# One pass for the gate-weighted biases, one turn and two DMAs for the softmax maxima, new orders

## The reference

```
h = token_block(x)                        # five taps, relu, batch norm
h = h + softmax_attention(layernorm(h))   # 8 heads of 16, +0.1 on a band
h = h + top2_experts(layernorm(h))        # 8 experts, hidden 256, gelu
h = h + linear_attention(layernorm(h))    # causal, elu + 1, 8 heads
h = h + experts(causal_attention(layernorm(h)))   # 8 experts, hidden 512
```

## Time and profile before

| | |
|---|---|
| median of three runs | 4315.55 us (4314.95, 4315.55, 4320.37) |
| span of the profiled execution, first to last instruction | 4319.1 us |
| its own time from outside | not listed by itself; the nearest run is 4320.37 us |
| PE busy | 4066.8 us, 41344 matmuls |
| DVE, ACT, POOL busy | 3367.6, 2784.5, 2596.6 us |
| token block | about the first 160 us |
| full rounds | 30 of about 125.6 us |

### The profile page before, as it was taken

The page is one execution under the profiler, slowest core; times in us unless marked ns, Lnnn a source line. Parts: engine busy times, 40 slices in busy tenths (PEclk is TensorE's granted clock), DMA queues, the critical chain, the costliest instruction groups (busy, mean ns, idle before and its releaser), DMA issues.

```text
span 4319.1 us, 104773 instructions
## 1 busy us (share of the span) xinstructions
PE 4066.8 (94%) x41344; PEld 3009.8 (70%) x41344; DVE 3367.6 (78%) x8878; ACT 2784.5 (64%) x4796; POOL 2596.6 (60%) x2494
## 2 busy tenths in 40 slices
PE   7678999999999999999999999999999999999998
PEld 3346777777777777777777777777777777777766
DVE  3357888888888888888888888878888887888876
ACT  3235766666676666667666666766666676666654
POOL 2034666666666666666666666666666666666656
PEclk9779999999999999999999999999999999999999
DMA  4200000011100001110000111000101100010000
GB/s 149 68 27 28 18 18 29 28 30 30 30 19 24 22 28 30 30 30 18 23 23 28 30 30 30 23 26 16 30 28 30 30 23 26 16 30 28 28 16 6
DMA packets 136939, 127.62 MB, mean 30 GB/s; under 512 B 28928, under 2 KB 135360, under 8 KB 136448
## 3 DMA queue, kind: packets, MB, share of 16 engines
q1 hardware_dynamic: 136448, 120.91, 9.6%
HBM read 71.05 MB, written 49.55 MB: 28 GB/s over the span
## 4 chain that ended last, share of the span: by engine, by line
PE 56%; DVE 24%; ACT 6%; POOL 5%; issue 4%; DMA 3%; SPq 2%; ACTq 0%; DVEq 0%; POOLq 0%
PE pf L1301 9%; PE pf L1303 8%; PE pf L1302 8%; PE pa L1561 8%; DVE h L1285 4%; PE pa L1447 3%; DVE hid_hi L1266 3%; PE pa L1543 3%; PE pa L1346 2%; PE pa L1433 2%; POOL inv_norm L650 2%; PE pa L1301 2%; ACT xn L726 2%; PE pa L1641 2%; PE pa L1303 2%
## 5 line engine op out<-in xcount | busy, mean ns | idle before, releaser
L660 POOL TENSOR_TENSOR hid_lo<-hid,hid_hi 128x504 f16<-128x504 f32 x1536 | 1835.5, 1212 | 775.8 <-DVE hid_hi L1266 775.8
L886 ACT ACTIVATE hid<-pf,vec 128x504 f32<-128x504 f32 x1536 | 1014.7, 680 | 505.5 <-PE pf L1303 356.9
L1301 PE MATMUL pf<-w_hi,hid_hi 128*126 128x128 f16 x6144 | 1133.7, 224 | 10.7 <-DVE h L1285 10.2
L1303 PE MATMUL pf<-w_hi,hid_lo 128*126 128x128 f16 x6144 | 1115.8, 221 | 0.0
L1302 PE MATMUL pf<-w_lo,hid_hi 128*126 128x128 f16 x6144 | 1115.4, 221 | 0.0
L1301 PEld LDWEIGHTS pf<-w_hi,hid_hi 128*126 128x126 f16 x6144 | 844.1, 137 | 153.5 <-issue 53.2
L1302 PEld LDWEIGHTS pf<-w_lo,hid_hi 128*126 128x126 f16 x6144 | 843.8, 137 | 28.5 <-issue 0.2
L1266 DVE CAST hid_hi<-hid 128x504 f16<-128x504 f32 x1536 | 845.4, 573 | 8.2 <-ACT hid L886 2.7
L1303 PEld LDWEIGHTS pf<-w_hi,hid_lo 128*126 128x126 f16 x6144 | 845.2, 138 | 0.0
L1285 DVE SCALAR_TENSOR_TENSOR h<-pf,gates,h 126x128 f32<-126x128 f32 x2048 | 574.1, 342 | 155.2 <-PE pf L1303 152.6
L616 POOL TENSOR_TENSOR pt<-pt,band 126x262 f32<-126x262 f32 x512 | 351.2, 707 | 527.6 <-ACT pt L773 527.4
(11 more groups left out here) (208 smaller groups left out, 7486.8 us busy)
## 6 DMA issues: line engine op xcount, KB each, us to landing
qk_spread<-terms SPq DMA_DIRECT2D x224, 126.0 KB, 2.5
qk_spread<-terms SPq DMA_DIRECT2D x192, 63.0 KB, 2.3
y_scratch<-hid SPq DMA_DIRECT2D x32, 252.0 KB, 2.1
y_in<-y_scratch SPq DMA_DIRECT2D x32, 252.0 KB, 3.2
terms<-qk_hi SPq DMA_DIRECT2D x32, 252.0 KB, 2.5
terms<-qk_lo SPq DMA_DIRECT2D x32, 252.0 KB, 2.6
qk_spread<-terms SPq DMA_DIRECT2D x32, 252.0 KB
terms<-ot_hi SPq DMA_DIRECT2D x32, 252.0 KB, 2.4
```

The costliest lines, as they stand in the source:

```text
L660: nc.gpsimd.tensor_tensor(hid_lo[:, c % 8], hid[:, c % HIDS], hid_hi[:, c % 8], ALU.subtract).then_inc(hid_lo_done[c % 2], 1)
L886: nc.scalar.activation(hid[:, c % HIDS], pf[:, c % 2, 0:TOK], func, bias=vec[:, bias:bias + 1]).then_inc(F["hid_ready"], 1)
L1301: nc.tensor.matmul(out, ah, bh, start=start, stop=False, skip_group_check=skip)
L1303: return nc.tensor.matmul(out, al, bh, start=False, stop=stop, skip_group_check=skip)
```

## The change

*Maxima.* `minus_max` becomes a 128 x 128 tile, and the 16 heads and sequences of maxima are its first 32 columns. One f16 matmul with the identity turns all of it; ACT copies the 32 rows to SBUF as f16; SP places 16 rows of 126 values each into row 3, and the other 16 into row 67 of the query tile, by two DMAs. The second pass of the scores waits for both. The four additions on DVE go.

*Biases.* The gates are written three times side by side (96 columns). Turned, rows 0 to 31 and 64 to 95 are the f16 high part, rows 32 to 63 the low part, which DVE makes by a subtraction (`gate_low`). `b2` is f16, with its high part in rows 0 to 63 and its low part in rows 64 to 95, and its rows hold zeros but for the columns of their own tile. So one f16 matmul of 96 rows and 512 columns gives high x high, low x high and high x low of all four tiles. `b2` is loaded within the token block: POOL zeroes an f32 staging tile, SP loads 12 small blocks (three in each of four iterations), POOL copies to f16 and subtracts for the low part.

*Orders.* All fifteen strings are new; of these PE's round is shown. Some semaphores share a name and count higher; that changes no wait.

```diff
-PE_ROUND = ("lhhoalhhaoaoloahlohloaoohlhhlaooahlahohalolhalahllaaoolahollhholallhhalaaolaoloahhaolahhlhoohaoo"
-            "laahlhhlaohaoohlolqhoohalolaaohaoohhhoqqqlholhalhloqlolhlolollhhlooqlhhqololhhoohhoolll")
+PE_ROUND = ("hhlahooqhaloaolhahlooolhohlhhloqahlaohaoahoalhhloohalhallaaloohllaalallaloaaohloalhaohlqaolooohl"
+            "ahhlahhoalhlhooaolhaaahooollohahhhoaoqqlhhoholhllloolhholohalhllohlqohlqolohllhoohhlool")
...
         # SP, in the token block's loop
+            def load_b2(i):
+                sp.wait_ge(b2_step, 1)
+                for part in range(3):
+                    first = part * G_ROWS + i * EXPERTS
+                    sp.dma_start(b2_wide[first:first + EXPERTS, :, i], b2_dram).then_inc(small_loaded, 16)
...
                 load_x(k + 1, 1)
                 store_y(k, 1)
+                if EARLY < k <= EARLY + TILES:
+                    load_b2(k - EARLY - 1)
...
         # SP, softmax_attention
+                for _ in range(8):
+                    yield
+                sp.wait_ge(S0["max_copied"], n(p + 1))
+                for r in range(2):
+                    sp.dma_start(q16[0][64 * r + MAX_ROW:64 * r + MAX_ROW + 1].rearrange("o g (t q) -> o (g t) q", t=TILES),
+                                 max_rows[16 * r:16 * r + 16]).then_inc(max_sent, 16)
...
         # POOL, after the constants
+            pool.wait_ge(w_lo_done, PIECES)
+            nc.gpsimd.memset(b2_wide, 0.0).then_inc(b2_step, 1)
+            pool.wait_ge(small_loaded, 32 + 16 * 3 * TILES)
+            nc.gpsimd.tensor_copy(b2[:], b2_wide).then_inc(b2_step, 1)
+            pool.wait_ge(b2_step, 2)
+            low_rows = slice(2 * G_ROWS, 3 * G_ROWS)
+            nc.gpsimd.tensor_tensor(b2[low_rows], b2_wide[low_rows], b2[low_rows], ALU.subtract).then_inc(b2_step, 1)
...
         # ACT
-                nc.scalar.copy(gate_t[a][:], pa[a][:, GATES_T[a], 0:TILE]).then_inc(SS[a]["gate_t_ready"], 1)
+                nc.scalar.copy(gate_t[a][0:3 * G_ROWS], pa[a][0:3 * G_ROWS, GATES_T[a], 0:TILE]
+                               ).then_inc(SS[a]["gate_t_high"], 1)
...
+                act.wait_ge(S0["max_turned"], n(p + 1))
+                nc.scalar.copy(max_rows[0:TILES * HEADS], pa0[0:TILES * HEADS, 0, 0:TILE]
+                               ).then_inc(S0["max_copied"], 1)
...
         # DVE, in front of each addition of a bias, and without the four additions
+            def gate_low(a, p):
+                dve.wait_ge(SS[a]["gate_t_high"], n(p + 1))
+                part = slice(G_ROWS, 2 * G_ROWS)
+                nc.vector.tensor_tensor(gate_t[a][part], pa[a][part, GATES_T[a], 0:TILE], gate_t[a][part],
+                                        ALU.subtract).then_inc(SS[a]["gate_t_ready"], 1)
...
-                for g in range(GROUPS):
-                    dve.wait_ge(S0["max_turned"], n(p * 4 + g + 1))
-                    nc.vector.tensor_tensor(q16[0][:, g], pa0[:, g % 3, 0:TOK], q16[0][:, g],
-                                            ALU.add).then_inc(S0["q_shifted"], 1)
...
         # PE
+                nc.tensor.matmul(pa[a][0:TILE, BIAS2[a]], gate_t[a][0:3 * G_ROWS],
+                                 b2[0:3 * G_ROWS, a].rearrange("p t d -> p (t d)"), start=True,
+                                 stop=True).then_inc(SS[a]["bias2_ready"], 1)
...
+                nc.tensor.matmul(pa0[:, 0, 0:TILE], minus_max[0:TILE], ident16[0:TILE, 0:TILE], start=True,
+                                 stop=True).then_inc(S0["max_turned"], 1)
...
-                pe.wait_ge(S0["q_shifted"], n(p * 4 + 4))
+                pe.wait_ge(max_sent, n.plain((p + 1) * 32))
```

More of the change, by code:

```diff
@@ L303, in program @@
         lsum = [sb(f"lsum{i}", [128, TILES]) for i in range(2)]
-        gate_t = [sb(f"gate_t{i}", [128, TILE]) for i in range(2)]
+        gate_t = [sb(f"gate_t{i}", [128, TILE], F16) for i in range(2)]
         y_in = sb("y_in", [128, TOK])
@@ L507, in softmax_attention @@
                     load_y(p + 1)
-                for _ in range(A0_STEPS):
+                for _ in range(8):
[4 more added lines that the diff above has]
+                                 max_rows[16 * r:16 * r + 16]).then_inc(max_sent, 16)
+                for _ in range(A0_STEPS - 8):
                     yield
@@ L529, in _ @@
             load_y(0)
-            sp.wait_ge(consts_built, 1)
-            for i in range(TILES):
-                sp.dma_start(b2[i * EXPERTS:(i + 1) * EXPERTS, :, i], b2_dram).then_inc(small_loaded, 16)
             run_rounds(softmax_queries_and_keys, softmax_attention, linear_and_causal_attention, hidden, output,
@@ L765, in softmax_attention @@
             def softmax_attention(p):
-                for _ in range(9):
+                for _ in range(8):
                     yield
+                act.wait_ge(S0["max_turned"], n(p + 1))
+                nc.scalar.copy(max_rows[0:TILES * HEADS], pa0[0:TILES * HEADS, 0, 0:TILE]
+                               ).then_inc(S0["max_copied"], 1)
+                yield
                 for g in range(8):
@@ L1012, in gate_top2 @@
                 nc.vector.tensor_tensor(over[0:TILE], other, mine, ALU.is_gt)
-                nc.vector.tensor_tensor(same[0:TILE], other, mine, ALU.is_equal).then_inc(S0["ranks2"], 1)
-                dve.wait_ge(S0["ranks2"], n(p + 1))
+                nc.vector.tensor_tensor(same[0:TILE], other, mine, ALU.is_equal).then_inc(S0["rank_step"], 1)
+                dve.wait_ge(S0["rank_step"], n(p * 4 + 1))
                 flat = earlier[0:TILE].rearrange("p a b -> p (a b)").unsqueeze(1).to_broadcast(
@@ L1365, in gate_bias2 @@
                 pe.wait_ge(SS[a]["gate_t_ready"], n(p + 1))
-                for i in range(TILES):
-                    last = nc.tensor.matmul(pa[a][0:TILE, BIAS2[a], i * D:(i + 1) * D], gate_t[a][:], b2[:, a, i],
-                                            start=True, stop=True)
-                last.then_inc(SS[a]["bias2_ready"], 1)
+                nc.tensor.matmul(pa[a][0:TILE, BIAS2[a]], gate_t[a][0:3 * G_ROWS],
+                                 b2[0:3 * G_ROWS, a].rearrange("p t d -> p (t d)"), start=True,
+                                 stop=True).then_inc(SS[a]["bias2_ready"], 1)
             def softmax_queries_and_keys(p):
@@ L1417, in softmax_attention @@
                 pe.wait_ge(S0["s_max"], n(p * 16 + 16))
-                for g in range(GROUPS):
-                    if g >= 3:
-                        pe.wait_ge(S0["q_shifted"], n(p * 4 + g - 2))
-                    for i in range(TILES):
-                        last = nc.tensor.matmul(pa0[:, g % 3, cols(i)], minus_max[0:TILE, i, g],
-                                                ident16[0:TILE, 0:TILE], start=True, stop=True)
-                    last.then_inc(S0["max_turned"], 1)
+                nc.tensor.matmul(pa0[:, 0, 0:TILE], minus_max[0:TILE], ident16[0:TILE, 0:TILE], start=True,
+                                 stop=True).then_inc(S0["max_turned"], 1)
                 yield
```

140 lines of the change are left out of this document (79 added, 61 removed).

## The result

The changed kernel takes 4478.19 us (median of 4 runs, 4467.91 to 4485.05), the kernel before 4317.96 us beside it: a ratio of 1.0357, 95% interval 1.0330 to 1.0383. It is slower by 3.6% where 2.1% less was forecast. The profiled execution took 4475.61 us, with a span of 4473.9.

What follows compares the result with a forecast made beforehand. TensorE's instruction stream was taken as the bound: 3.12 us gained in each of 30 full rounds, 93.6 us, less 1.7 us at both ends, gave 92 us off 4315.55, so 4224 us; range 4178 to 4296.

Steps and rivals of the forecast that it cites:

- What bounds the kernel: Whole round: TensorE's instruction stream in written order is the bound; a microsecond less per round is worth 30 us.
- The turn and the biases: TensorE's turning matmuls and bias matmuls become one f16 matmul each: gains of 1.33 us and 1.54 us per round.
- The wait before the second bias: TensorE's wait for ScalarE's copy goes, since two output steps, 1.38 us, cover a 0.97 us chain: 0.35 us gained.
- The new way of the maxima: Turn, copy and two DMAs before second-pass scores: 3.7 us chain under 3.8 us of work, so zero wait.
- Rivals 3 and 4: Maxima DMAs land at twice the median, 4293 us, chance 0.06; or longest issue and landing, 4336 us, chance 0.06.
- What the order takes back: Between last raw scores and the turn, less work stands in the new order: 0.1 us lost per round.
- Both ends: First and end rounds and input loop: 3.8 and 1.8 us gained, 2.3 and 5 lost, net 1.7 us lost.
- Rival 1: A pair's linear and causal attention fills the round by itself; only 34 us come off, 4282 us, chance 0.13.
- Rival 5: Some wait that the new orders make takes the whole gain: about 4315 us, chance 0.04.

Runs made afterwards that it cites:

- 9: Kernel before, third of the three passes left out in every hidden step (10.1 us less TensorE work a round): 4274.10 us, ratio 0.9901.
- 10: Kernel before, third pass left out in every second hidden step (5.0 us less TensorE work a round): 4287.53 us, ratio 0.9931.
- kernel 6: Changed instructions in the old orders, low step early, steps exchanged to give the loads and maxima DMAs more room: 4330.74 us, ratio 1.0025.
- 8: Kernel before, turn of the second gates ahead of two output steps, two output steps ahead of the second and third raw scores: 4321.96 us, ratio 0.9994.
- 2: Kernel before, its instructions kept, with all fifteen order strings of the change: 4498.14 us, ratio 1.0416.
- 12: Changed kernel in its new orders, squares held back until first gates are written, low step early, second gates' turn and copy one hidden step earlier: 4433.91 us, ratio 1.0259.
- 1: Changed kernel with the old order strings, three letters moved: 4444.78 us, ratio 1.0292.
- 13: Kernel before, GpSimd's root in the linear and causal attention replaced by a multiplication: 4302.69 us, ratio 0.9968.
- 14: Kernel before with two-pass hidden steps and GpSimd's root replaced by a multiplication: 4248.30 us, ratio 0.9849.
- 4: Changed kernel with sixteen unread f16 matmuls of 512 columns ahead of TensorE's wait for the first gates: 4449.99 us, ratio 1.0303.

## Why the prediction was wrong

Two steps failed: the price of TensorE's work, by which the gain did not come, and the charge for the new orders, by which a loss came in its place.

**What bounds the kernel: the first step that failed.** "A microsecond less of TensorE's work or waiting per round is worth 30 us" was read from 97% busy. Runs 9 and 10 put it at 4 to 6 us. In this order, whose waits are short, TensorE's work is cover for the other engines' steps, and its high busy share tells how full it is, not that the time follows it. The chain of waits had pointed that way: TensorE had 56% of it (by itself still far above the seventh measured), and the prediction took the other 44% for short waits in TensorE's stream. Its condition, "as long as the next step's operands are there", was then checked only at the steps that change.

**The turn and the biases.** The terms were right as holds: 0.21 us forecast for a bias, 0.22 measured. Per round, TensorE's busy time fell from 121.5 us to 0.955 x 125.40 = 119.7 in kernel 6, which has all the change's instructions at full clock: 1.8 us, less than the 2.9 that the holds gave. Part of the difference is in the reading: 0.34 of the 1.39 us held by the turns was a wait, which was never busy time. The rest is not explained by a run.

**The wait before the second bias.** "It gains 1.8 us a round, which I count as nothing", and 1.38 us of cover for a chain of 0.97. The chain was right by its parts, the queue in front of it was not looked at: TensorE waits up to 0.8 us for the low step in the new orders, and in the old ones 2.3 us. Behind the wait nothing was won even where it was covered (8).

**The new way of the maxima.** Forecast a chain of 3.7 us with a landing of 2.4; the landing is 1.8, and the scores wait only now and then (5.4 us in 9 of 28 rounds). Rivals 3 and 4, long landings, are out. The rule of the Trainium skill that was weighed there ("DMA: Bandwidth & Descriptors", Specifications) speaks of full rate; that the landing would double was the prediction's own estimate, and their landing is shorter in its median than the shortest of the earlier trace rows.

**What the order takes back: the second step that failed.** 0.1 us a round was charged, from the steps next to the turn. The new orders cost 183 us with the old instructions (2). All five queues had been remade, and the prediction walked TensorE's at three places, SP's and ScalarE's at one, and no queue of VectorE's beside GpSimd's. Of the change's 5.0 us a round, idle time is 4.3 more and the same instructions as in 6 are busy 122.2 - 119.7 = 2.5 us longer, which fits the lower clock: some 160 us at half of it in the stretch 560 to 4050 cost about 80 us, or 3 a round; against that stand 1.8 us of work saved. Of the idle time, 3.4 us is the wait for the first gates. How the rest of the 183 us splits over the orders stays open (holding back the squares gave 58 us of the change's loss back, and 12 did not settle the rest).

**Both ends.** Charged with 1.7 us lost; the stretch up to the first norm became 5.3 us shorter. Two parts came as forecast: TensorE's weight loads wait 35.0 us for input loads where 29.6 were the earlier trace rows, 5.4 more where 5 were charged, and the wait at the loop's end is 6.2 us instead of 7.88, 1.7 less for 1.8. That the whole is shorter is not shown to be the new instructions' doing: with them in the old orders the first norm starts at 383.8 (1) and 374.8 (6), with the old ones in the new orders at 368.1 (2).

**The rivals.** Rival 1 foresaw that TensorE would not be the bound, with one chain in its place; 13 and 14 give that chain a share only. Rival 5, a wait that the new orders make, had the right place for the cause, a chance of 0.04 and a price that ended at the whole gain: nothing bounded it there. In the changed kernel the waits cost their own length and, with the clock that fell behind them, some 2.5 us a round more.

## What to carry to other kernels

Before work removed from a busy engine is priced, ask what waits under it: make the same work shorter everywhere in the kernel as it is and see how much of it the time returns. When orders are remade, walk every queue, and beside it the engines that contend with it. A new step is as early as its place in its queue, not as its operand.

## What the runs showed of the hardware

A VectorE instruction of 126x256 with two f32 operands in SBUF takes 0.42 us alone and up to 2.00 beside a GpSimd instruction, all of it recorded as busy; it ends 0.3 us after GpSimd's. A cast from f32 to f16, with one operand, is held too: it takes 0.41 us in the median of nine between 2040 and 2062 us of the changed kernel, 1.35 at the most. After 3.4 us of idle TensorE is granted 0.5 of its clock for some 3 us, and not where the wait is filled (4); waits of 0.83, 0.60 and 0.19 us between f32 matmuls of 126 and 252 columns come ahead of 6 us at 0.5 in the same kernel 4. DMAs of 252-byte runs land in 1.8 us, loads of 1008-byte runs into the same tile in 2.4. GpSimd's power of 126x16 elements takes 3.0 us, its multiplication 0.32.
